# Reordering one DMA queue's window of loads in a two-batch Mamba block with adaptive layer norm

## The chip, the cores and the metric

The kernel runs on one core of one Trainium2 chip. The metric is the device time of one execution in microseconds (us). Five engines matter here: TensorE (PE in the profile; PEld is its weight load), VectorE (DVE), ScalarE (ACT), GpSimd (POOL) and SyncE (SP). SP computes nothing in this kernel. It is the queue on which nearly every DMA is issued, one after the other, each behind the semaphore waits written ahead of it.

## The reference

Input x is 2 batches of 2048 rows of 512. A small modulation vector gives shifts, scales and gates. Then two residual steps follow:

```
h = layernorm(x) * (1 + ca) + sa
x = x + ga * mamba(h)          # in_proj 512->2x1024, conv of 4 taps, silu, x_proj, dt_proj, softplus,
                               # scan s = s*exp(dt*A) + dt*h*B over time for 1024 channels x 16 states,
                               # y = sum_n s*C + h*D, y *= silu(gate), out_proj 1024->512
h = layernorm(x) * (1 + cb) + sb
x = x + gb * (sum_r h @ factors[r] / sqrt(8) + bias)
```

All data is float32.

## The kernel before, in words

The rows are cut into 16 chunks of 256 rows (`CHUNKS`), eight for each batch. Every engine's program is a loop over 16 rounds, one a chunk. In round c the four compute engines do the scan of chunk c, 64 units of two channel tiles by one state. They go through it in 32 steps (`s`) of two units. Woven into the same steps are the front part of chunk c+1 (input projection, convolution, silu, the dt, B and C projections) and the back part of chunk c-1 (gate, output projection, second norm and linear layer). What runs at which step is written out by hand for each engine.

The scan of a unit goes as follows. ACT makes the decay into one of three PSUM banks (L724). POOL makes dt*h*B for four units at a time (L570). DVE runs the scan (L1432). The product with C is made by DVE for some units (`sc_d`, a ring of three tiles, L1447) and by POOL for the others (`state_p`, L598). PE transposes and sums all products into `y_bank` (L1012).

PE's program at steps 1 to 7 of a round is what the change bears on. At s = 1, 2, 3, 4 and then 7, 8, 9, 10 it runs `project_h(c+1, q, j)` (L1087), which needs weight tile m = 2q + j of the input projection in `win_h`, a ring of three tiles. At s = 0, 1, 2 it ends the gate projection of chunk c-1 (`project_gate`, L1059, weight tiles in `win_z`, also a ring of three). At s = 4, 5, 6, 7 it runs `turn_sums(c-1, q)` (L1143). Behind each `turn_sums` DVE has a `gate_sums` (L1528): two at s = 6, one at s = 7, one at s = 8. At s = 6 PE runs the first convolution taps (L1070). ACT waits for them at s = 7 before its tanh.

The weight tiles do not stay in SBUF. For each chunk SP loads all eight `win_h` tiles (`load_h`, L359) and all eight `win_z` tiles (`load_z`, L371), 256 KB each. Because the rings hold three tiles, the load of tile m waits until the tile three before it has been used: `load_h(c+1, 3)` waits for `project_h` of tile 0 (s = 1), `load_z(c, 2)` waits for `project_gate` of the last tile of chunk c-1 (s = 2). SP further loads the B and C rows of a chunk, broadcast to all partitions (`load_b` L337, `load_c` L347, 1 MB a half), the input rows for the first norm (`load_xa`, L434, 512 KB) and for the residual (`load_xc`, L428, 512 KB), and stores the output (`store_out`, L501). SP's order is fixed by its `one_round` (L436 on); a wait there holds back everything written after it.

Of the kernel before, what the change touches and what calls it, by code (L numbers as in the profile page):

```python
# [34 lines left out]
KE = E // P  # L35
# [17 lines left out]
H_TILES, Z_TILES = 3, 3  # L53
# [65 lines left out]
def products_after(unit):  # L119
    return DVE_COUNT[unit]  # L120
# [41 lines left out]
def build(nc, x, win_m, xp_t, dt_t, wo_t, chan, cond_t, wmod, factors, bias, out):  # L162
# [11 lines left out]
    with ExitStack() as ctx:  # L174
# [144 lines left out]
        def _(sp):  # L319
# [5 lines left out]
            def store_bc(c, par):  # L325

                sp.wait_ge(a_free[1], A_FREES * c + 4)
                sp.dma_start(bc_dram[par].rearrange("i (n r) -> (i n) r", n=N), bc_s[:, :]).then_inc(bc_stored, 16)

            def load_b(c, par, h):  # L330

                if c:
                    sp.wait_ge(ub_made, QUADS * c - 2 * (1 - h) - 1)
                sp.wait_ge(bc_stored, 16 * c + 16)
                n0 = h * N // 2
                src = bc_dram[par, 0:1, n0 * ROWS:(n0 + N // 2) * ROWS].to_broadcast([P, N * ROWS // 2])
                sp.dma_start(b_all[:, n0:n0 + N // 2, :].rearrange("p n r -> p (n r)"), src).then_inc(b_loaded[h], 16)  # L337

            def load_c(c, par, h):

                if c:
                    sp.wait_ge(multiplied, products_after(UNITS * c - (1 if h else N // 2 + 1)))
                    sp.wait_ge(pooled, QUADS * c - 2 * (1 - h))
                sp.wait_ge(bc_stored, 16 * c + 16)
                n0 = h * N // 2
                src = bc_dram[par, 1:2, n0 * ROWS:(n0 + N // 2) * ROWS].to_broadcast([P, N * ROWS // 2])
                sp.dma_start(c_all[:, n0:n0 + N // 2, :].rearrange("p n r -> p (n r)"), src).then_inc(c_loaded[h], 16)  # L347

            def load_h(c, m):
                i = KE * c + m  # L350
                if c == CHUNKS:
                    return
                if i >= H_TILES:
                    (c0, m0) = divmod(i - H_TILES, KE)
                    if m0 % 2:
                        sp.wait_ge(a_full[m0 // 2 % 2], A_JOBS[m0 // 2 % 2] * c0 + 2 + m0 // 4)
                    else:
                        sp.wait_ge(h_used, PAIRS * c0 + m0 // 2 + 1)
                sp.dma_start(win_h[i % H_TILES][:, :, :], win_m[m]).then_inc(h_loaded[i % H_TILES], 16)  # L359

            def load_z(c, m):
                i = KE * c + m
                if i >= Z_TILES:
                    (c0, m0) = divmod(i - Z_TILES, KE)
                    if m0 % 2 and c0 == FINAL:
                        sp.wait_ge(a_full[m0 // 2 % 2], a_jobs + 1 + m0 // 4)
                    elif m0 % 2:
                        sp.wait_ge(c_full[m0 // 2 % 2], C_JOBS * c0 + 1 + m0 // 4)
                    else:
                        sp.wait_ge(z_used, PAIRS * c0 + m0 // 2 + 1)  # L370
                sp.dma_start(win_z[i % Z_TILES][:, :, :], win_m[KE + m]).then_inc(z_loaded[i % Z_TILES], 16)  # L371
# [41 lines left out]
            def store_wo(i):  # L413

                sp.wait_ge(wo_kept, i + 1)
                sp.dma_start(wo_dram[i], spare[2].rearrange("p t d -> p (t d)")).then_inc(wo_stored, 16)

            def store_ffn(i):

                sp.wait_ge(ffn_kept, i + 1)  # L420
                sp.dma_start(ffn_dram[i], spare[0].rearrange("p t d -> p (t d)")).then_inc(ffn_stored, 16)

            def load_xc(c):

                if c == 0:
                    sp.wait_ge(ffn_scaled, HALVES)
                wait(sp, out_stored, 16 * c)
                sp.dma_start(xc[:, :, :], rows_of(x_rows, c)).then_inc(xc_loaded, 16)  # L428

            def load_xa(c):  # L430

                for j in range(2):
                    sp.wait_ge(a_full[j], A_JOBS[j] * (c - 1) + 1)
                sp.dma_start(xa[:, :, :], rows_of(x_rows, c)).then_inc(xa_loaded, 16)  # L434

            def one_round(c, par, la, lc):  # L436
                if c >= 2:
                    store_out(c - 2)
                if c:
                    load_z(c - 1, 7)  # L440
                load_z(c, 0)
                if la is not None:
                    load_h(c + 1, 3)
                if c:
                    load_c(c, par, 1)
                load_z(c, 1)
                if la is not None:
                    load_h(c + 1, 4)
                load_z(c, 2)
                if la is not None:  # L450
                    load_h(c + 1, 5)
                    load_h(c + 1, 6)
                if c >= 2:
                    load_xc(c - 1)
                if c + 2 < CHUNKS:
                    load_xa(c + 2)
                if c == PER + 1:

                    sp.wait_ge(c_full[0], C_JOBS * PER)
                    sp.wait_ge(c_full[1], C_JOBS * PER)  # L460
                    sp.wait_ge(ffn_stored, 16 * HALVES)
                    sp.dma_start(ffn[:, :, :].rearrange("p (i k) d -> p i (k d)", i=HALVES),
                                 ffn_dram.rearrange("i p f -> p i f")).then_inc(ffn_loaded, 16)
                if la is not None:
                    load_h(c + 1, 7)
                    if c == 1:
                        store_ffn(0)
                    for m in range(H_TILES):
                        load_h(c + 2, m)
                    if c == 1:  # L470
                        store_ffn(1)
                        load_xc(0)
                    if c == 0:

                        sp.wait_ge(rows_made, 2 * BATCH)
                        for b in range(BATCH):
                            sp.dma_start(bias_gate[b:b + 1, :], gb[0:1, b, :]).then_inc(bias_gated, 16)
                        for i in range(PAIRS):
                            store_wo(i)
                    if c == PER:  # L480

                        sp.wait_ge(c_full[0], C_JOBS * (PER - 1) + 5)
                        sp.wait_ge(c_full[1], C_JOBS * (PER - 1) + 5)
                        sp.wait_ge(wo_stored, 16 * PAIRS)
                        sp.dma_start(wo[:, :, :].rearrange("p (i k) d -> p i (k d)", i=PAIRS),
                                     wo_dram.rearrange("i p f -> p i f")).then_inc(wo_loaded, 16)
                    store_bc(c + 1, 1 - par)
                    load_b(c + 1, 1 - par, 0)
                for m in (3, 4):
                    load_z(c, m)  # L490
                if la is not None:
                    load_b(c + 1, 1 - par, 1)
                    load_c(c + 1, 1 - par, 0)
                for m in (5, 6):
                    load_z(c, m)

            def store_out(c):

                for t in range(LB):
                    sp.wait_ge(c_free[t], C_JOBS * (c + 1))  # L500
                sp.dma_start(rows_of(out_rows, c), xc[:, :, :]).then_inc(out_stored, 16)  # L501

            rounds(one_round)
            load_z(FINAL, 7)
            store_out(FINAL - 1)
# [1230 lines left out]
```

## Time and profile before

| | us |
|---|---|
| median of 3 runs | 2046.96 |
| lowest, highest | 2046.85, 2053.15 |
| the profiled execution, its own time | 2046.96 |
| span of that execution in the trace | 2045.2 |
| busy in the span: DVE, POOL | 1865.8 (91%), 1834.8 (90%) |
| busy in the span: PE, ACT | 1775.0 (87%), 1514.3 (74%) |
| DMA queue of SP, share of 16 engines | 24.9% |

The time is the slowest (here the only) core's. The span runs from the first to the last instruction in the trace. The 1.8 us between the two lie outside it. A round lasts about 122 us. Engine busy shares are averages over the whole span, so they don't say what is waited for in a given step; the rows below do. Line numbers are those of the kernel before. Times in a row of the timeline are from the start of the span. A row may merge several like instructions (x4, x8), and square brackets hold the engine's idle time ahead of the row and what ended it. A row of windows gives the stretch, its length, then the busy time (and instructions) of PE, PEld, DVE, ACT and POOL in this order, then the granted clock of PE as a share of full speed, the busy share of the DMA engines and GB/s. A row of DMA issues ends with the KB of one and the us from issue to landing.

### The profile page before, as it was taken

Reading aid. Unit: us, or ns where it says so; the run is one execution under the profiler, and the core shown is the slowest. Engines: PE = TensorE matmul, PEld = TensorE weight load, DVE = VectorE, ACT = ScalarE, POOL = GpSimd, SP = SyncE. Lnnn points to the kernel's source line nnn. Section 1 sums busy time; section 2 is a strip of 40 time slices with the busy share of each in tenths; the row PEclk is TensorE's granted clock in tenths of the full one; section 3 lists DMA queues with packets and bytes.
Section 4 is the critical chain, followed back from the end, with each engine's and each line's share of the span. In section 5 each row is a group of like instructions: output and inputs, shape, how many; then the busy total and the mean of one; then the engine's idle time right before and its main releaser. Section 6 shows DMA issues by size and latency. Waiting matters only on the chain. (4 is left out here: it accounts for less than half of the span.)

```text
span 2045.2 us, 29343 instructions
## 1 busy us (share of the span) xinstructions
PE 1775.0 (87%) x9128; PEld 1317.7 (64%) x9128; DVE 1865.8 (91%) x2240; ACT 1514.3 (74%) x4646; POOL 1834.8 (90%) x925
## 2 busy tenths in 40 slices
PE   7976988989888888998989898898988889898698
PEld 5655757666575766757566675766657576675564
DVE  2899999999999999899999999999999999999995
ACT  3767778787877868678786877878687786877663
POOL 1789999998999999899999989999999999999992
PEclk9898999999999999999999999999999999999898
DMA  4656404032130402204032240403214040220300
GB/s 169 248 103 175 125 32 159 17 135 62 64 132 20 158 21 104 93 27 160 12 145 86 90 135 22 156 20 130 67 60 137 22 155 21 104 68 28 118 27 31
DMA packets 72001, 186.17 MB, mean 91 GB/s; under 512 B 6818, under 2 KB 8482, under 8 KB 63908
## 3 DMA queue, kind: packets, MB, share of 16 engines
q1 hardware_dynamic: 68148, 176.95, 24.9%
q0 software_dynamic: 3696, 7.34, 2.2%
q8 instruction: 73, 1.20, 0.2%
q14 instruction: 84, 0.69, 0.1%
HBM read 172.20 MB, written 12.06 MB: 90 GB/s over the span
## 5 line engine op out<-in xcount | busy, mean ns | idle before, releaser
L570 POOL TENSOR_TENSOR ub<-u,b_all 128x2048 f32<-128x2048 f32 x255 | 1160.3, 4550 | 46.7 <-DMA b_all<-bc_scratch 45.5
L724 ACT ACTIVATE decay<-dt,decay_rate 128x256 f32<-128x256 f32 (+1 forms) x2048 | 889.6, 466 | 32.9 <-DVE state_p L1432 30.5
L1432 DVE TENSOR_TENSOR_SCAN decay<-decay,carry,ub 128x512 f32<-128x512 f32 x610 | 761.9, 1276 | 27.2 <-ACT decay L724 26.1
L598 POOL TENSOR_TENSOR state_p<-state_p,c_all 128x1024 f32<-128x1024 f32 (+1 forms) x256 | 498.9, 1949 | 110.4 <-ACT carry L708 108.8
L1432 DVE TENSOR_TENSOR_SCAN state_p<-decay,carry,ub 128x512 f32<-128x512 f32 x414 | 527.5, 1274 | 20.3 <-ACT decay L724 18.6
L1012 PE MATMUL y_bank<-ident,sc_d 128*128 128x128 f32 x2440 | 367.3, 286 | 96.3 <-DVE sc_d L1447 96.0
L1012 PEld LDWEIGHTS y_bank<-ident,sc_d 128*128 128x128 f32 x2440 | 298.7, 148 | 175.9 <-DVE sc_d L1447 142.7
L1447 DVE TENSOR_TENSOR sc_d<-decay,c_all 128x512 f32<-128x512 f32 x610 | 407.0, 671 | 4.0 <-DMA c_all<-bc_scratch 3.9
L708 ACT ACTIVATE carry<-decay 128x2 f32<-128x2 f32 x610 | 100.6, 165 | 322.8 <-DVE sc_d L1447 322.8
L1012 PE MATMUL y_bank<-ident,state_p 128*128 128x128 f32 x1656 | 234.4, 281 | 52.4 <-POOL state_p L598 51.2
L1012 PEld LDWEIGHTS y_bank<-ident,state_p 128*128 128x128 f32 x1656 | 193.9, 144 | 123.6 <-POOL state_p L598 99.2
L1087 PE MATMUL bank_a<-hT,win_h 128*128 128x256 f32 x992 | 238.5, 384 | 24.4 <-DVE hc L1496 22.1
L1059 PE MATMUL bank_c<-hT,win_z 128*128 128x256 f32 x960 | 231.0, 387 | 0.0
L1159 PE MATMUL bank_c<-wo,yg 128*128 128x512 f32 x480 | 223.3, 593 | 0.0
L1087 PEld LDWEIGHTS bank_a<-hT,win_h 128*128 128x128 f32 x992 | 182.2, 192 | 48.7 <-DVE hc L1496 25.4
L1059 PEld LDWEIGHTS bank_c<-hT,win_z 128*128 128x128 f32 x960 | 182.3, 194 | 29.7 <-issue 6.7
L1159 PEld LDWEIGHTS bank_c<-wo,yg 128*128 128x128 f32 x480 | 85.2, 190 | 66.0 <-issue 64.6
L1189 PE MATMUL bank_c<-ffn,hT 128*128 128x512 f32 x240 | 125.8, 627 | 0.0
L1070 PE MATMUL bank_a<-pre_z,tap_diag 128*128 128x256 f32 x496 | 118.8, 382 | 1.9 <-DVE bank_a L1487 1.9
L1003 PE MATMUL y_bank<-ident,skipped 128*128 128x128 f32 x256 | 42.8, 293 | 80.9 <-ACT y_rows L813 80.9
L1070 PEld LDWEIGHTS bank_a<-pre_z,tap_diag 128*128 128x128 f32 x496 | 92.7, 192 | 26.1 <-issue 13.4
L720 ACT ACTIVATE decay<-ident 128x1 f32<-128x1 f32 x608 | 103.4, 170 | 0.1
(139 smaller groups left out, 1844.4 us busy)
## 6 DMA issues: line engine op xcount, KB each, us to landing
win_h<-win_m SPq DMA_DIRECT2D x128, 256.0 KB, 2.7
win_z<-win_m SPq DMA_DIRECT2D x128, 256.0 KB, 2.8
b_all<-bc_scratch SPq DMA_DIRECT2D x31, 1024.0 KB, 4.7
c_all<-bc_scratch SPq DMA_DIRECT2D x31, 1024.0 KB, 6.6
xa<-x SPq DMA_DIRECT2D x16, 512.0 KB, 5.1
xc<-x SPq DMA_DIRECT2D x16, 512.0 KB, 3.8
out<-xc SPq DMA_DIRECT2D x15, 512.0 KB, 3.8
ffn<-factors POOLq DMA_DIRECT2D x7, 1024.0 KB, 10.4
```

The lines of the kernel that those rows point to most:

```text
L570: pool.tensor_tensor(ub[:, slot, :, :, :], u[:, (PAIRS * c + q) % U_PAIRS, :, :].unsqueeze(1).to_broadcast([P, QUAD, 2, ROWS]), b_all[:, n ...
L598: pool.tensor_tensor(part, part, c_all[:, n + QUAD - k:n + QUAD, :].unsqueeze(2).to_broadcast([P, k, 2, ROWS]), ALU.mult).then_inc(pooled, 1)
L720: act.activation(bk[:, ROWS:ROWS + 1], ident[:, 0:1], ACT.Copy, scale=0.0)
L724: last = act.activation(bk[:, j * ROWS + j:(j + 1) * ROWS], dt[:, pair % DT_PAIRS, j, j:], ACT.Exp, scale=decay_rate[:, e, n:n + 1])
L1012: last = pe.matmul(y_bank[:, at:at + P], tile[:, j, t * P:(t + 1) * P], ident[:, :], start=False, stop=last_of_pair, is_transpose=True, sk ...
L1059: last = pe.matmul(dst[:, j * ROWS:(j + 1) * ROWS], tile[:, k, :], hTc[:, k, :], start=(k == 0), stop=(k == KD - 1))
L1070: last = pe.matmul(h_lane(c, q)[:, j * ROWS:(j + 1) * ROWS], tap_diag[:, i, 2 * q + j, :], pre[q % 2][:, j, k:k + ROWS], start=False, stop ...
L1087: last = pe.matmul(h_lane(c, q)[:, j * ROWS:(j + 1) * ROWS], win_h[i % H_TILES][:, k, :], hT[c % H_RING][:, k, :], start=(k == 0 and j == ...
L1159: last = pe.matmul(bank_c[t][:, :], yg[:, k, t * P:(t + 1) * P], wo[:, k, :], start=(k == 0), stop=(k == KE - 1))
L1189: last = pe.matmul(bank_c[t][:, :], hT[c % H_RING][:, k, t * P:(t + 1) * P], ffn[:, k, :], start=False, stop=(k == KD - 1))
L1432: dve.tensor_tensor_scan(dst, bk[:, :], ub[:, quad % UB_RING, i, :, :].rearrange("p j r -> p (j r)"), carried_in[:, n, 2 * q:2 * q + 1], A ...
L1447: dve.tensor_tensor(sc_d[:, i % D_RING, :, :], bk[:, :].rearrange("p (j r) -> p j r", j=2), c_all[:, n:n + 1, :].to_broadcast([P, 2, ROWS] ...
```

## The change

Only SP's `one_round` is altered. The loads and stores are the same ones, with the same waits, sizes and counts. Their order at the start of a round changes: the second half of C and the last gate tile come first, then the store of the finished chunk, then the gate tiles 0 to 2, then the rows for the residual and for the norm (and in one round the reload of `ffn`). Only then come the `win_h` tiles 3 to 7, which before were placed in between.

```
             def one_round(c, par, la, lc):
+                if c:
+                    load_z(c - 1, 7)
+                    load_c(c, par, 1)
                 if c >= 2:
                     store_out(c - 2)
-                if c:
-                    load_z(c - 1, 7)
-                load_z(c, 0)
-                if la is not None:
-                    load_h(c + 1, 3)
-                if c:
-                    load_c(c, par, 1)
-                load_z(c, 1)
-                if la is not None:
-                    load_h(c + 1, 4)
-                load_z(c, 2)
-                if la is not None:
-                    load_h(c + 1, 5)
-                    load_h(c + 1, 6)
+                for m in range(Z_TILES):
+                    load_z(c, m)
                 if c >= 2:
                     load_xc(c - 1)
                 if c + 2 < CHUNKS:
                     load_xa(c + 2)
...
                 if la is not None:
-                    load_h(c + 1, 7)
+                    for m in range(H_TILES, KE):
+                        load_h(c + 1, m)
                     if c == 1:
                         store_ffn(0)
                     for m in range(H_TILES):
```

SP's rows of one middle round before, from the gate tiles 5 and 6 that end a round (the first row holds these two) to the `win_h` tiles of the next; `out<-xc` is the store, `xc<-x` and `xa<-x` the two loads of rows:

```order
L371 DMA win_z<-win_m 128x512 x2
L501 DMA out<-xc 128x2x512
L371 DMA win_z<-win_m 128x512 x2
L359 DMA win_h<-win_m 128x512
L347 DMA c_all<-bc_scratch 128x2048
L371 DMA win_z<-win_m 128x512
L359 DMA win_h<-win_m 128x512
L371 DMA win_z<-win_m 128x512
L359 DMA win_h<-win_m 128x512 x2
L428 DMA xc<-x 128x2x512
L434 DMA xa<-x 128x2x512
L359 DMA win_h<-win_m 128x512 x4
```

The same stretch of SP's program after the change, whose first row is those two gate tiles and tile 7:

```order
L371 DMA win_z<-win_m 128x512 x3
L347 DMA c_all<-bc_scratch 128x2048
L493 DMA out<-xc 128x2x512
L371 DMA win_z<-win_m 128x512 x3
L428 DMA xc<-x 128x2x512
L434 DMA xa<-x 128x2x512
L359 DMA win_h<-win_m 128x512 x8
```

The first `win_h` load of the round, tile 3, stood ahead of `c_all` and of the gate tiles 1 and 2. It now stands behind all of them and behind both loads of rows. `c_all` and the gate tile 7 moved to the front, and the store behind them.

## Rows read from the trace of the kernel before

**Rows 1.** Busy by window in us: round 4, then round 1.
```profile
569.00:691.00 122.00, 107.16 (x566) 79.74 (x565) 114.42 (x138) 94.04 (x289) 114.07 (x59) 0.99 0.24 83
199.00:326.00 127.00, 108.59 (x563) 80.78 (x563) 116.49 (x142) 95.14 (x296) 122.95 (x66) 0.97 0.33 103
```

**Rows 2.** Waits of DVE, whole span: us in total, times, longest.
```profile
DVE sc_d L1447 <- DMA c_all<-bc_scratch: 3.9, 6, 1.4
```

**Rows 3.** SP's issues at the start of round 4: start, length, us.
```profile
570.12 2.06 SPq L371 DMA_DIRECT2D win_z<-win_m  x2
576.96 0.33 SPq L359 DMA_DIRECT2D win_h<-win_m  x1
577.39 0.37 SPq L347 DMA_DIRECT2D c_all<-bc_scratch  x1
578.68 0.33 SPq L371 DMA_DIRECT2D win_z<-win_m  x1
...
582.58 0.33 SPq L371 DMA_DIRECT2D win_z<-win_m  x1
...
585.61 2.49 SPq L359 DMA_DIRECT2D win_h<-win_m  x2
...
588.68 0.41 SPq L434 DMA_DIRECT2D xa<-x  x1
```

**Rows 4.** From issue to landing: those of 576.96, 578.68, 587.77 and 588.68.
```profile
win_h<-win_m SPq DMA_DIRECT2D x1, 256.0 KB, 3.3
...
win_z<-win_m SPq DMA_DIRECT2D x1, 256.0 KB, 5.1
...
win_h<-win_m SPq DMA_DIRECT2D x1, 256.0 KB, 2.5
...
xa<-x SPq DMA_DIRECT2D x1, 512.0 KB, 5.1
```

**Rows 5.** PE's timeline, round 4, steps 2 to 7.
```profile
580.65 1.89 PE L1059 MATMUL bank_c<-hT,win_z 128*128 128x256 f32 x8
...
585.86 1.89 PE L1087 MATMUL bank_a<-hT,win_h 128*128 128x256 f32 x8
...
589.33 0.60 PE L1143 MATMUL bank_c<-ident,y_rows 128*128 128x128 f32 x4
...
597.12 1.99 PE L1087 MATMUL bank_a<-hT,win_h 128*128 128x256 f32 x8 [1.71 <-DVE hc L1496]
```

**Rows 6.** DVE's timeline: twice round 4, then rounds 6 and 13.
```profile
583.25 0.69 DVE L1447 TENSOR_TENSOR sc_d<-decay,c_all 128x512 f32<-128x512 f32 x1 [0.90 <-DMA c_all<-bc_scratch]
...
591.65 1.28 DVE L1528 TENSOR_TENSOR yg<-bank_c,yg 128x512 f32<-128x512 f32 x2
...
834.82 1.28 DVE L1528 TENSOR_TENSOR yg<-bank_c,yg 128x512 f32<-128x512 f32 x2
...
1682.72 1.27 DVE L1528 TENSOR_TENSOR yg<-bank_c,yg 128x512 f32<-128x512 f32 x2
```

**Rows 7.** SP's issue of gate tile 2 in rounds 6 and 13.
```profile
825.26 0.33 SPq L371 DMA_DIRECT2D win_z<-win_m  x1
...
1674.66 0.33 SPq L371 DMA_DIRECT2D win_z<-win_m  x1
```

**Rows 8.** POOL's last product of round 3.
```profile
568.25 1.26 POOL L598 TENSOR_TENSOR state_p<-state_p,c_all 128x512 f32<-128x512 f32 x1
```

**Rows 9.** Gate tile 2 of round 1: issue to landing, us.
```profile
win_z<-win_m SPq DMA_DIRECT2D x1, 256.0 KB, 8.1
```

**Rows 10.** PE after two idle stretches.
```profile
562.69 0.66 PE L1012 MATMUL y_bank<-ident,sc_d 128*128 128x128 f32 x4 [2.60 <-DVE sc_d L1447]
...
665.53 0.63 PE L1003 MATMUL y_bank<-ident,skipped 128*128 128x128 f32 x4 [2.32 <-ACT y_rows L813]
```

**Rows 11.** Windows at 562.69 and after 665.53, with the granted clock.
```profile
558.00:569.00 11.00, 7.52 (x48) 6.39 (x47) 10.70 (x11) 10.13 (x34) 8.37 (x7) 1.00 0.79 305
...
666.60:670.00 3.40, 3.40 (x12) 2.25 (x11) 3.40 (x5) 2.17 (x8) 3.24 (x6) 0.50 0.00 0
```

## The prediction

> **What bounds the kernel now.** I read the busy time by window first, for a middle round. In 122 us DVE is busy 114.42 and POOL 114.07, against 107.16 for PE [rows 1]. So DVE has about 7.6 us of idle time in a round, and what holds DVE up in the middle of a round is passed on to the end almost whole. Then I read DVE's waits. The only DMA that DVE waits for in the steady rounds is the second half of C, 3.9 us in 6 waits [rows 2]. That is all this change could win from DVE directly. Then I followed SP's queue, PE and DVE through the first seven steps of round 4, because only there the order of the issues changes.
>
> Before, the weight tile 3 (call it h3) is issued at 576.96, right after `project_h` of tile 0, and lands 3.3 us later, at 580.3 [rows 3, 4]. PE uses it at 585.86 [rows 5]. It is 5.6 us early. In SP's queue the second half of C follows at 577.39 [rows 3] and lands when DVE's product at 583.25 is let go, after a wait of 0.90 us [rows 6].
>
> **The change, part by part.**
>
> *C earlier.* The load waits for the last products of the round before. POOL's ends at 569.5 [rows 8], and gate tile 7, which stays ahead of it, is issued at 570.12 [rows 3]. So C goes out at about 570.5, 6.9 us earlier, and DVE no longer waits for it. On its own this is worth at most the 3.9 us of [rows 2]. These waits lie ahead of the place where I find the loss, and that place is tied to PE and the DMA, not to DVE's earlier work. So I count the gain as nothing where the loss below occurs. Bounds: 0 to -3.9 us.
>
> *Store later, gate tiles together.* The store goes out at about 571, behind C. It has until about 583, when the load into its buffer is reached, so `out_stored` holds nobody back. Gate tiles 1 and 2 keep their own waits on PE and their times, 578.68 and 582.58 [rows 3]. Nobody needs tiles 0 to 2 before step 26. Price 0.
>
> *The `win_h` tiles later.* This is the term that counts. h3 now stands behind gate tile 2, and that waits for PE's last gate matmul. That one starts its run at 580.65 and is 1.89 us long [rows 5], so SP is free at 582.58. Behind it come the two loads of rows, 512 KB each, and only then h3. With the spacing of SP's issues (0.43 to 0.53 us) h3 goes out at about 584.0. But issue is not landing. The transfers of this queue land in order and share one path. The gate tile issued at 578.68 took 5.1 us and landed at 583.8, just 0.55 us behind C [rows 3, 4, 6]. So a queued 256 KB costs about 0.6 us. For the rows I take the same three transfers as they run before. The `win_h` load that ends the pair of 585.61 is issued at 587.77 and lands after 2.5 us at 590.3. The row load of 588.68 lands after 5.1 us at 593.8 [rows 3, 4]. From the first issue to the landing of the second row load that is 6.0 us, of which 3.5 are the two row loads. After the change gate tile 2 stands in that first place. I take 6.15, since landings are given to a tenth only and the first of the three may be slowed by what is ahead of it, and 0.65 for h3 behind: **h3 lands 6.8 us after the issue of gate tile 2**, here at 589.4, instead of 580.3. PE wants it at 585.86 and so stands still for 3.5 us.
>
> What is queued behind that wait on PE: the four matmul pairs of tile 3, `turn_sums` 0, the turns of step 5, `turn_sums` 1 (which starts 3.47 us after the tile-3 matmuls do and is 0.60 long, so it is done 4.07 us after h3 is in), then the taps [rows 5]. DVE waits for the two `turn_sums` with its two `gate_sums` of step 6. They start at 591.65, and the second at 592.25 (two in 1.28 us, [rows 6]). With h3 at 589.4 the second can start at 589.45 + 4.07 = 593.5, which is 1.3 us later. The first is let go at 591.8, no loss. The next things behind it have room: PE's tile 4 waits 1.71 us for DVE anyway [rows 5]. The taps (eight like matmuls, 1.89 us as the other rows of eight in [rows 5]) end at about 595.3, ACT's tanh and the copies behind them are some 3 us of work before the next decay that DVE needs two units later, so that they are in time by an estimated 1 us. So round 4 loses 1.3 us at full clock.
>
> The same sum for the twelve rounds 2 to 13: issue of gate tile 2 + 6.8 + 4.1 minus the start of the second `gate_sums`. The least is round 6, 825.26 + 10.9 against 835.4, 0.7 us [rows 6, 7]. The most is about that of round 13, 1674.66 + 10.9 against 1683.3, 2.25 us [rows 6, 7]. The twelve average 1.85. Together **22 us**.
>
> - Round 9 has the 1 MB reload of `ffn` ahead of h3 as well. By the 3.5 us of the two row loads this is another 3.5, less what rounding leaves: +3 us.
> - Round 14 has no load for the norm; 1.75 less, so about +0.5.
> - In round 1 gate tile 2 takes 8.1 us to land [rows 9], 5.3 more than the usual 2.8 of the page, so h3 is up to 4.9 us too late for DVE (1.3 + 5.3 - 1.75, no load for the residual yet). But there POOL is busy for 122.95 of 127 us [rows 1] and DVE has room against it. Bounds 0 and +4.9; I take +1.5.
> - Rounds 0 and 15: in round 0 h3 still waits for `project_h` of tile 0; in 15 there is none. 0.
>
> Sum at full clock 22 + 3 + 0.5 + 1.5 = 27 us.
>
> *The clock.* PE now stands still for about 3.5 us in each of these rounds. Rows show both answers: after 2.60 us idle PE went on at 1.00 (2.4 GHz), after 2.32 us its clock was 0.50 (1.2 GHz) for 3.4 us from 666.60 [rows 10, 11]. The new stand is longer than both. If PE resumes at half clock, the 4.07 us between h3 and `gate_sums` grow by up to 1.7 us (half of 3.4). Bounds 0 and 13 x 1.7 = 22 us. Since a drop may begin in the idle time and may stay out, I take 8.
>
> The Trainium skill ("TensorE: Matmul & The Clock Gate", section on HAM oscillation) says that a loop in which PE waits for a DMA between its bursts falls back to the half clock each time. By that rule the clock term would be at its upper end, 22 us. The trace agrees after the 2.32 us and not after the 2.60.
>
> **Sum:** the profiled execution took 2046.96 us, the median of the runs itself, with 1.8 us outside the span. 2047 + 27 + 8 = **2082 us**, 1.7% slower.
>
> **The rivals.**
>
> *A. Late, and as priced* (forecast): 2070 to 2092.
>
> *B. The burst lands early and only the gain is left.* This decides at one point: h3 must be there 4.07 us ahead of the second `gate_sums`, in round 4 at 588.2, which is 5.6 us after gate tile 2's issue instead of 6.8. If the loads of rows overlapped h3 so that it landed 2.7 us after its own issue, it would be in at 586.7 and nobody would be late. The waits for C go: 2047 - 3.9 = 2043. Against it: the landings in order, 0.55 us apart, in [rows 3, 4, 6]. The skill ("DMA: Bandwidth & Descriptors", Anatomy of one DMA) gives 2.0 us plus bytes over 436 GB/s. For the 1.5 MB from gate tile 2 to h3 this makes 5.6 us as an estimate, just at the point, and by it most rounds would lose well under 1 us; the rows here show 6.0 for 1.25 MB, slower than its 5.0, and I go by them.
>
> *C. Every resumption is at half clock:* 27 + 22 = 49, so 2096.
>
> *D. DVE makes good half of it.* DVE has 7.6 us of idle time in a round [rows 1], and if half the delay falls into waits that end on POOL or ACT work that was not delayed, 27 becomes 14: 2061. Against it: most of those waits end on ACT, which itself follows DVE.
>
> **How the numbers follow.** A 0.62, C 0.12, D 0.14, B 0.12. No change means within 0.3%, 6 us, about what a measurement of this kernel can tell. B is nearly all "same" (2043 is 0.2% less), with a little for faster. So faster 0.03, same 0.09, slower 0.88. The range leaves out B and the far end of C: 2058 to 2098.
>
> **What would show it.** In the profile after: h3's issue at about 14 us into a round's start instead of 7; a new wait of PE's L1087 for DMA `win_h`, 13 to 14 times, 3 to 4 us each, about 45 to 50 us in all, longest in round 9 or 1; a new wait of DVE's L1528 for PE L1143, some 22 us or more; DVE's wait for `c_all` gone; more stretches of PEclk 0.5. The prediction is wrong if L1087 waits for the DMA less than 2 us a time, or if DVE's L1528 does not wait although PE does.

## The result, and the profile after

The changed kernel takes 2102.22 us in the median of 4 runs (2098.09 to 2106.25), against 2046.9 before. The ratio is 1.0265, with a 95% interval of 1.0231 to 1.03: slower by 2.65%, where 1.7% was forecast, and 4 us beyond the upper end of the range. The direction and the mechanism were as forecast; the size was not.

The profiled execution took 2098.99 us, with a span of 2097.3 us, 52.1 more than before. The first lines of its page:

```profile
span 2097.3 us, 29343 instructions
...
PE 1794.1 (86%) x9128; PEld 1338.2 (64%) x9128; DVE 1866.6 (89%) x2240; ACT 1514.9 (72%) x4646; POOL 1833.7 (87%) x925
```

DVE, ACT and POOL do the same work in the same busy time. PE is busy for 19.1 us longer with the same 9128 matmul records: it ran a larger part of them at half clock (the mean granted clock of the span is 0.955, against 0.968 before). So the 52 us are idle time of DVE and POOL. The waits say which; first DVE's, then PE's for a DMA (us in total, times, longest):

```profile
DVE yg L1520 <- PE bank_c L1135: 62.1, 27, 6.0
...
DVE hc L1488 <- ACT tanh_s L781: 20.9, 16, 2.1
```

```profile
PE bank_a L1079 <- DMA win_h<-win_m: 53.4, 14, 6.6
```

(`gate_sums` is L1520 now, `turn_sums` L1135, `project_h` L1079, the gate projection L1051.) Neither the 62.1 nor the 53.4 us were in the trace before, and the wait of DVE for `c_all` [rows 2] is gone. The wait of `hc` was there, with 23.8 us. The 62.1 us are 10 more than the span grew; 3.9 of these are the waits for C. The other 6 are smaller waits of DVE that shrank, such as that of `hc`. So little of the delay was made good.

Round 4 again, SP's issues as in [rows 3]:

```profile
581.93 0.33 SPq L371 DMA_DIRECT2D win_z<-win_m  x1
582.37 0.37 SPq L347 DMA_DIRECT2D c_all<-bc_scratch  x1
582.84 0.39 SPq L493 DMA_DIRECT2D out<-xc  x1
583.66 10.48 SPq L371 DMA_DIRECT2D win_z<-win_m  x3
594.18 0.43 SPq L428 DMA_DIRECT2D xc<-x  x1
594.71 1.31 SPq L434 DMA_DIRECT2D xa<-x  x1
596.07 8.03 SPq L359 DMA_DIRECT2D win_h<-win_m  x4
```

The last row holds tile 3, issued at 596.07, with tiles 4 to 6. From issue to landing, the second load of rows and tile 3:

```profile
xa<-x SPq DMA_DIRECT2D x1, 512.0 KB, 5.8
...
win_h<-win_m SPq DMA_DIRECT2D x1, 256.0 KB, 5.1
```

So tile 3 is in at 601.2, 0.6 us behind the rows. PE and DVE in that stretch, as in [rows 5, 6]:

```profile
601.18 2.56 PE L1079 MATMUL bank_a<-hT,win_h 128*128 128x256 f32 x8 [3.93 <-DMA win_h<-win_m]
603.53 1.06 PE L1135 MATMUL bank_c<-ident,y_rows 128*128 128x128 f32 x4
604.38 1.78 PE L1004 MATMUL y_bank<-ident,state_p 128*128 128x128 f32 x8
606.00 0.60 PE L1004 MATMUL y_bank<-ident,sc_d 128*128 128x128 f32 x4
606.43 0.60 PE L1135 MATMUL bank_c<-ident,y_rows 128*128 128x128 f32 x4
...
611.96 0.48 PE L1079 MATMUL bank_a<-hT,win_h 128*128 128x256 f32 x1 [1.01 <-DVE hc L1488]
```

```profile
604.63 0.69 DVE L1520 TENSOR_TENSOR yg<-bank_c,yg 128x512 f32<-128x512 f32 x1 [2.68 <-PE bank_c L1135]
607.07 0.69 DVE L1520 TENSOR_TENSOR yg<-bank_c,yg 128x512 f32<-128x512 f32 x1 [1.75 <-PE bank_c L1135]
```

PE stands (sits idle, waiting) for 3.93 us, and then its eight records of tile 3, two for each of four matmuls, take 2.56 us instead of 1.89 and the transposes behind them 1.06 instead of 0.60. The windows from tile 3's first matmul to the second `gate_sums`, in rounds 4, 5 and 6, show the granted clock of each:

```profile
601.18:607.07 5.89, 5.89 (x29) 5.38 (x30) 1.46 (x3) 1.08 (x4) 5.81 (x6) 0.71 0.22 66
726.79:733.64 6.85, 6.85 (x29) 6.02 (x30) 1.46 (x3) 1.08 (x4) 6.77 (x6) 0.61 0.15 48
853.60:857.81 4.21, 4.21 (x29) 3.95 (x30) 1.75 (x3) 1.12 (x5) 4.13 (x5) 1.00 0.34 85
```

At clock 1.00 the same 29 matmul records take 4.21 us, which is the 4.07 of the forecast and the hand-over to DVE; at 0.71 they take 5.89 and at 0.61 they take 6.85. I read this stretch in all 14 rounds that wait: 4.2 us in rounds 6, 12 and 14, 5.9 in rounds 2, 4, 8 and 10, 6.3 in round 1, and 6.9 to 7.1 in the six odd rounds 3 to 13. Over 4.2 that is 25 us in all. The clock was low for 50.5 us of these stretches, and half of that is the same 25.

The stretch is 5.9 us or about 7 by how long the clock stays low. These are the low stretches of rounds 4 and 5:

```profile
602.48:605.89 3.41, 3.41 (x16) 3.04 (x15) 0.69 (x1) 0.58 (x2) 3.41 (x3) 0.50 0.28 76
725.36:732.18 6.82, 5.39 (x17) 4.56 (x18) 2.89 (x4) 2.27 (x8) 6.74 (x6) 0.50 0.31 109
```

In round 4 the clock fell 1.3 us after PE had gone on, and stayed low for 3.4 us. In round 5 it fell 1.4 us before PE went on, while PE stood, and stayed low for 6.8 us, 5.4 of them behind the wait.

### The profile page after: what moved, and what is told of

Read it like the earlier page. It is cut to its first block, busy times and chain, and to the rows that moved or that the text cites. A ratio compares the mean times of both kernels' runs of the same rounds, so it can differ in the third digit from the quotient of the medians.

```text
span 2097.3 us, 29343 instructions
## 1 busy us (share of the span) xinstructions
PE 1794.1 (86%) x9128; PEld 1338.2 (64%) x9128; DVE 1866.6 (89%) x2240; ACT 1514.9 (72%) x4646; POOL 1833.7 (87%) x925
## 4 chain that ended last, share of the span: by engine, by line
PE 16%; DVE 11%; ACT 9%; issue 7%; POOL 6%; DMA 2%; SPq 0%; DVEq 0%; ACTq 0%; POOLq 0%
DVE decay L1424 4%; PE bank_a L1079 4%; PE y_bank L1004 3%; ACT decay L716 3%; POOL ub L562 3%; DVE state_p L1424 3%; POOL state_p L590 3%; DVE sc_d L1439 2%; DMA win_h<-win_m 2%; PE bank_c L1051 2%; PE bank_c L1151 1%; PE bank_c L1181 1%; ACT dt L829 1%; ACT hT L731 1%; PE bank_a L1062 1%
## 5 line engine op out<-in xcount | busy, mean ns | idle before, releaser
L1079 PE MATMUL bank_a<-hT,win_h 128*128 128x256 f32 x992 | 254.0, 403 | 69.4 <-DMA win_h<-win_m 53.4
L1004 PE MATMUL y_bank<-ident,state_p 128*128 128x128 f32 x1656 | 240.1, 286 | 41.3 <-POOL state_p L590 40.2
L1004 PEld LDWEIGHTS y_bank<-ident,state_p 128*128 128x128 f32 x1656 | 202.0, 148 | 109.0 <-POOL state_p L590 82.0
L1079 PEld LDWEIGHTS bank_a<-hT,win_h 128*128 128x128 f32 x992 | 190.2, 201 | 99.9 <-DMA win_h<-win_m 56.7
L1051 PE MATMUL bank_c<-hT,win_z 128*128 128x256 f32 x960 | 232.5, 389 | 0.0
L1051 PEld LDWEIGHTS bank_c<-hT,win_z 128*128 128x128 f32 x960 | 183.1, 195 | 29.9 <-issue 6.7
L781 ACT ACTIVATE tanh_s<-bank_a 128x512 f32<-128x512 f32 x62 | 36.7, 592 | 123.3 <-PE bank_a L1062 122.8
```

The lines of the kernel that those rows point to most:

```text
L1004: last = pe.matmul(y_bank[:, at:at + P], tile[:, j, t * P:(t + 1) * P], ident[:, :], start=False, stop=last_of_pair, is_transpose=True, sk ...
L1051: last = pe.matmul(dst[:, j * ROWS:(j + 1) * ROWS], tile[:, k, :], hTc[:, k, :], start=(k == 0), stop=(k == KD - 1))
L1079: last = pe.matmul(h_lane(c, q)[:, j * ROWS:(j + 1) * ROWS], win_h[i % H_TILES][:, k, :], hT[c % H_RING][:, k, :], start=(k == 0 and j == ...
```

## The experiments

Each ratio is to runs of the kernel before taken beside the experiment. Their median was 2048 us for e1 to e4, 2049 us for e5 and e6 and 2051 us for e7 and e8.

**Only tile 3 moved back** (e1), from the changed kernel:

```
                 for m in range(Z_TILES):
                     load_z(c, m)
+                    if m == 0 and la is not None:
+                        load_h(c + 1, 3)
...
-                    for m in range(H_TILES, KE):
+                    for m in range(H_TILES + 1, KE):
```

> The changed kernel with one load moved back: weight tile 3 of the input projection stands behind gate tile 0 again, all else in the changed order. Theory (only tile 3 being late costs anything): PE waits for no win_h DMA in the rounds 2 to 14, DVE's wait of the gate_sums for PE falls from 62 us to under 2, and the time is that of the kernel before or up to 4 us less, 2043 to 2048. Rival (the store and the C load at the front, or tiles 4 to 7 behind the row loads, carry part of the loss): over 2060, with a new wait of PE for tiles 4 to 7.

2041.98 us, 1 us under the expected, ratio 0.997 (0.9957 to 0.9982). PE waits for no `win_h` load at all, and DVE for `turn_sums` once:

```profile
DVE yg L1522 <- PE bank_c L1137: 0.4, 1, 0.4
```

One load of 256 KB a round, at a wrong place, carries the whole loss. The store, C, the rows and the tiles 4 to 7 stayed where the change had put them.

**Only the tiles late** (e3), from the kernel before: `load_h(c+1, 3)` to `(c+1, 6)` taken out of their places and put, with tile 7, behind the loads of rows.

```
                     load_z(c - 1, 7)
                 load_z(c, 0)
-                if la is not None:
-                    load_h(c + 1, 3)
                 if c:
                     load_c(c, par, 1)
                 load_z(c, 1)
-                if la is not None:
-                    load_h(c + 1, 4)
                 load_z(c, 2)
-                if la is not None:
-                    load_h(c + 1, 5)
-                    load_h(c + 1, 6)
...
-                    load_h(c + 1, 7)
+                    for m in range(H_TILES, KE):
+                        load_h(c + 1, m)
```

> The kernel before with only tiles 3 to 6 moved behind the two loads of rows; the store and the C load keep their old places. Theory (the tiles carry all of it): about the changed kernel, 2095 to 2108, and DVE's waits for C, 3.9 us, stay or move. Rival (C and the store at the front carry a part of the 52 us): 2060 to 2085.

2107.39 us, ratio 1.0286 (1.026 to 1.0312), with the two waits of the changed kernel:

```profile
PE bank_a L1081 <- DMA win_h<-win_m: 57.1, 14, 6.3
```

```profile
DVE yg L1522 <- PE bank_c L1137: 61.9, 27, 6.3
```

With e1 this is both halves: the late tiles are enough for the loss, and tile 3 is needed for it. DVE's waits for C are gone here too, although C was not moved: DVE comes to them later.

**Tile 3 ahead of the rows** (e2), from the changed kernel: behind gate tile 2, but ahead of the two row loads.

```
                 for m in range(Z_TILES):
                     load_z(c, m)
+                if la is not None:
+                    load_h(c + 1, 3)
                 if c >= 2:
                     load_xc(c - 1)
...
-                    for m in range(H_TILES, KE):
+                    for m in range(H_TILES + 1, KE):
```

> The changed kernel with tile 3 directly behind gate tile 2 and ahead of the two loads of rows. Theory (the bytes in front of tile 3 are what makes it late, not the waits that its issue stands behind): tile 3 lands about 0.6 us behind gate tile 2, some 3.4 us after that one's issue, just when PE wants it; PE waits under 0.5 us a round, round 1 excepted; 2045 to 2052. Rival (standing behind the wait for the last gate matmul is the cost in itself): PE still stands 2 us or more a round, over 2070.

2044.54 us, ratio 0.9977 (0.9964 to 0.9991). The time is 0.5 us under the expected. PE's waits for the load are 7.0 us, most of it in round 1; the four others are of 0.2 to 0.9 us, where under 0.5 was expected:

```profile
PE bank_a L1081 <- DMA win_h<-win_m: 7.0, 5, 4.9
```

Tile 3 landed 3.2 to 4.3 us after the issue of gate tile 2 in rounds 2 to 14. So standing behind the wait for the last gate matmul costs nothing that the time shows; the 1 MB of rows in front does.

**One load of rows ahead** (e7): tile 3 between the two.

```
+                if la is not None:
+                    load_h(c + 1, 3)
                 if c + 2 < CHUNKS:
                     load_xa(c + 2)
...
-                    for m in range(H_TILES, KE):
+                    for m in range(H_TILES + 1, KE):
```

> The changed kernel with tile 3 between the two loads of rows: one load of 512 KB ahead of it instead of two. Theory (loss = lateness less DVE's room of about 1.7 us, plus half clock if PE stands long): tile 3 lands 5.0 to 5.4 us after gate tile 2 is issued, PE stands about 1.8 us in rounds 2 to 14, DVE waits 0 to 0.7 us a round there and up to 5 in round 1, the clock seldom drops behind so short a stand; DVE's wait for turn_sums is 6 to 14 us in all and the time 2046 to 2056. Rival (loss goes with the stand of PE, 1.8 of 3.6 us gives half of it): about 2072.

2059.15 us, ratio 1.0046 (1.0029 to 1.0063), about 9 us slower than before; the profiled one's span is 2059.0. The rival's 2072 is out, but my 2046 to 2056 was missed as well, and DVE's wait was 24.3 us instead of 6 to 14. The reason is mostly the clock: I had expected it to hold behind so short a stand. It was low for 21.1 us of the stretches up to the second `gate_sums`, in rounds 1, 3, 4, 11 and 12; less half of that, DVE's wait is 13.8 us, inside 6 to 14. Tile 3 also landed less evenly than expected, 4.7 to 6.7 us after gate tile 2 in rounds 2 to 14. Rounds 3 and 6, first PE, then the windows:

```profile
467.92 3.18 PE L1081 MATMUL bank_a<-hT,win_h 128*128 128x256 f32 x8 [1.88 <-DMA win_h<-win_m]
...
836.36 0.92 PE L1081 MATMUL bank_a<-hT,win_h 128*128 128x256 f32 x3 [1.80 <-DMA win_h<-win_m]
```

```profile
467.92:473.82 5.90, 5.90 (x29) 5.17 (x30) 3.51 (x5) 2.88 (x10) 5.82 (x5) 0.71 0.54 175
836.36:840.58 4.22, 4.22 (x29) 3.95 (x30) 3.50 (x5) 2.96 (x10) 4.14 (x4) 1.00 0.72 239
```

Two stands of like length, one followed by a drop and one not. In rounds where the clock held, DVE waited for 1.1 us less than PE had stood: 0.72 after 1.80, 0.38 after 1.46. That is DVE's room: so much later can PE's sums come without holding DVE up.

**PE late, but never idle** (e6), from the kernel before: 8 matmuls of zeros ahead of tile 3, whose loads keep their place. They add zero to a half bank that the next matmuls fill. The zero tile is written once, by GpSimd at the start.

```
+                if c >= 2 and 2 * q + j == 3:
+                    pe.wait_ge(zeroed, 1)
+                    for _ in range(8):
+                        pe.matmul(h_lane(c, q)[:, j * ROWS:(j + 1) * ROWS], zeros[:, :],
+                                  hT[c % H_RING][:, 0, :], start=False, stop=False, ...)
                 pe.wait_ge(h_loaded[i % H_TILES], 16 * (i // H_TILES + 1))
```

> The kernel before, its DMA order untouched, with 8 such matmuls of zeros ahead of tile 3: PE is late by 8 x 0.43 = 3.5 us at full clock, with no stand still and no DMA wait. Theory (lateness at full clock costs 3.5 us less the room that DVE has, about 1.7 us on the average, in 13 to 14 rounds): DVE waits 22 to 27 us more at the gate_sums and the time is 2068 to 2075. Rival (DVE makes good half of it later in the round): 2055 to 2062. Rival (lateness alone gives all the 52 us): 2090 or more.

2067.91 us, ratio 1.0099 (1.0072 to 1.0127), as the first theory had it, at the lower end of its 2068 to 2075. The zeros (two records for each matmul), tile 3 behind them, and the clock up to the second `gate_sums`:

```profile
590.17 3.62 PE L1091 MATMUL bank_a<-hT,zeros 128*128 128x256 f32 x16
593.63 1.89 PE L1095 MATMUL bank_a<-hT,win_h 128*128 128x256 f32 x8
```

```profile
593.60:597.70 4.10, 4.10 (x30) 3.82 (x30) 2.31 (x3) 1.69 (x6) 4.02 (x5) 1.00 0.19 59
```

```profile
DVE yg L1536 <- PE bank_c L1151: 26.0, 27, 1.5
```

Being 3.5 us late at full clock costs 20.6 us of span (2065.8 against 2045.2), not 52.

**The stand filled** (e5), from the changed kernel: the same edit with 7 matmuls of zeros, 3.0 us, ahead of the wait for the late tile 3.

> The changed kernel, with 7 matmuls of a zero weight tile (they add zero to the half bank that is filled next) on PE ahead of its wait for tile 3, in chunks 2 to 15. They take about 7 x 0.43 = 3.0 us, less than PE stood still there in nearly every round, so that PE is busy while it waits and tile 3 is used at the same time. Theory (about 26 of the 52 us are PE running at 1.2 GHz after the stand): the clock stays at 1.00 behind the wait, the stretch from the tile-3 matmuls to the second gate_sums is 4.2 us in all rounds instead of 4.2 to 7.1, DVE's wait for turn_sums falls from 62 us to about 36, and the time to 2070 to 2078. Rival (the drops would have come anyway, or matmuls of zeros do not hold the clock): 2095 or more, with the same drops.

2086.43 us, ratio 1.0191 (1.0166 to 1.0215) against 1.0265 for the changed kernel, whose intervals do not meet: more work for PE, and a faster kernel. Rounds 4 and 13, PE and then the windows:

```profile
598.75 1.99 PE L1087 MATMUL bank_a<-hT,win_h 128*128 128x256 f32 x8 [0.75 <-DMA win_h<-win_m]
...
1716.80 3.42 PE L1087 MATMUL bank_a<-hT,win_h 128*128 128x256 f32 x8 [1.92 <-DMA win_h<-win_m]
```

```profile
598.75:602.97 4.22, 4.22 (x29) 3.95 (x30) 1.62 (x4) 1.08 (x4) 4.14 (x5) 1.00 0.26 73
1716.80:1722.70 5.90, 5.90 (x29) 5.14 (x30) 0.69 (x1) 0.86 (x3) 5.90 (x3) 0.71 0.19 48
```

In 12 of the 14 rounds the stretch is 4.1 to 4.2 us at clock 1.00. Only in rounds 1 and 13, where PE still stood for 3.62 and 1.92 us, did it drop; in round 9 it held although PE stood for 2.69 us. But the time is above my 2070 to 2078, and DVE waits 47.1 us, not 36. Low clock in that stretch fell from 50.5 to 6.8 us, worth 22 us by half. Against this tile 3 landed 5 us later in the sum of the rounds (6.9 to 8.4 us after gate tile 2 in rounds 2 to 13, round 9 left out, against 6.4 to 7.3). The net 17 is near the 15 that DVE's wait fell by; of these the span shows 12 (2085.3 against 2097.3). Why the loads are slower in this kernel I did not find out.

**More filling** (e8): 9 matmuls, 3.9 us.

> The changed kernel with 9 matmuls of zeros ahead of the wait for tile 3 instead of 7: 9 x 0.43 = 3.9 us, so that PE hardly stands still at all and what is lost is lateness at full clock alone. Theory: no low clock between tile 3 and the second gate_sums except in round 1, DVE's wait for turn_sums 36 to 46 us, 2076 to 2086, not slower than with 7 although PE gets up to 0.9 us more work in front of tile 3 in some rounds. Rival (the filling itself delays tile 3 by as much as it saves): 2090 or more.

2085.64 us, ratio 1.0162 (1.0143 to 1.0181), DVE's wait 46.3 us. PE stands for 6.7 us in all, 2.33 of them in round 1 and 2.96 in round 9, where tile 3 landed 10.2 us after gate tile 2. In both rounds the clock fell; for round 9 I had not expected it. In the seven rounds in which the zeros cover the whole of the lateness DVE waits 2.44 us; that is 3.9 less a room of 1.45. From 7 to 9 matmuls nothing more is to be gained that this measurement tells apart.

**Only C first** (e4), from the kernel before:

```
             def one_round(c, par, la, lc):
+                if c:
+                    load_z(c - 1, 7)
+                    load_c(c, par, 1)
                 if c >= 2:
                     store_out(c - 2)
-                if c:
-                    load_z(c - 1, 7)
                 load_z(c, 0)
                 if la is not None:
                     load_h(c + 1, 3)
-                if c:
-                    load_c(c, par, 1)
                 load_z(c, 1)
```

> The kernel before with only the C load and gate tile 7 at the front of the round, the store behind them, the win_h tiles in their old places. Theory (the C waits of DVE are real but small): DVE's 3.9 us of waits for c_all go and the time is 2043 to 2047, 0 to 0.2% less than before. Rival (a later store or an earlier C collides with another transfer): 2050 or more, with a new DMA wait on some engine.

2041.67 us, 1.3 us under the expected, ratio 0.9974 (0.9961 to 0.9988). DVE waits for no `c_all` load any more, and the span is 2040.4 us, 4.8 less than before. So the first part of the change is good for 0.26% by itself. e4 and e1 are both faster than the kernel before, by a little that the intervals still show, and than the changed one; between the two nothing can be told.

## Why the prediction was right or wrong

- *What would break, and where.* Right. Tile 3 late behind the rows, PE standing at step 4, DVE at its two `gate_sums` of step 6. e1, e2 and e3 show that there is no second cause.
- *When tile 3 lands.* Forecast 6.8 us after gate tile 2 is issued, measured 6.4 to 7.3 in rounds 2 to 8 and 10 to 13, 9.2 in round 9, 4.8 in round 14, 10.0 in round 1. Right in the main, and it ruled out rival B. The estimate by the formula of the Trainium skill ("DMA: Bandwidth & Descriptors", Anatomy of one DMA), 5.6 us, was too low: the page gives it for one DMA issued by GpSimd, and here it was used for four in a row on SP's queue. e2 shows that an early landing would indeed have cost nothing.
- *Lateness at full clock.* Forecast 27 us after the 3.9 of C, so 31 of DVE's wait. Measured 62.1 less 25 of clock, 37. Short by 6. About 4 of these are round 1, taken at 1.5 with a bound of 4.9: PE stood there for 6.60 us and DVE for 7.4, 1.7 of it by the low clock, and the other 5.7 are outside the bound. About 2 are the landing, 7.0 us on the average of rounds 2 to 13 without round 9, not 6.8. The room of DVE came to about 1.7 us a round (3.5 less 1.85), read from the kernel before, where DVE had itself been held up on the way. In e1, without the waits for C, the second `gate_sums` starts 5.4 us after tile 3 does in rounds 2 to 14, which less 4.1 is a room of 1.3; e7 and e8 show 1.1 to 1.45. Over twelve rounds this comes to about 5 us, nearly all of it the 3.9 of C just counted.
- *The clock.* This is the step that failed. I took 8 us and bounded it at 22. It cost 25 us of DVE's wait. The bound came from one drop of 3.4 us per round. In the odd rounds 3 to 13 the low clock lasted for 6.8 us, long enough to cover nearly the whole stretch from tile 3 to the second `gate_sums`: 0.61 in the window of round 5, where a single such drop gives the 0.71 of round 4. The middle value rested on the hope that a drop would begin in the idle time and so cost less. In these six rounds it did begin there, 0.95 to 1.44 us before PE went on, and cost more: 2.6 to 2.9 us each, against 1.7 for the drops of rounds 2, 4, 8 and 10 that began behind it. e6 and e5 show that it is the stand that brings the drops, not the lateness: with PE late but busy there is none in 14 of 14 and 12 of 14 rounds.
- *Rival C*, every resumption at half clock, gave 2096 and named the right mechanism. It got 0.12 where it should have had most. The rule of the Trainium skill ("TensorE: Matmul & The Clock Gate", section on HAM oscillation) spoke for it: PE waits for a DMA in each round and falls back each time. The trace after agrees in 11 of 14 rounds; in 6, 12 and 14 the clock held.
- *Rival D*, DVE makes good half: wrong. Of 62.1 us of new waits 52.1 reached the span, and 3.9 of the rest are C.
- *The gain of C.* Right in size (3.9 forecast at most, 4.8 us of span in e4, and single runs of the kernel before differ by more than that) and right that the changed kernel would not see it: e3, without it, is at 1.0286 (1.026 to 1.0312) against 1.0265 (1.0231 to 1.03), which can't be told apart.

The sum as measured: 37 (late at full clock) + 25 (clock) - 3.9 (the waits for C, which have gone over into the 37) - 6 (other waits of DVE that shrank) = 52 us. Without the clock this is 27, the forecast to the microsecond, and that is partly luck: 6 too few for round 1 and the landing, 6 that other waits gave back. By this account the 17 us between 2082 and the 2099 of the profiled execution are the clock, 25 instead of 8; the median of the runs lies 3 us above that execution.

## What to carry to other kernels

In a queue whose loads land in order (in each of the ten traces here, all 409 DMAs of SP's queue landed in the order of their issue), count the bytes in front of each load up to the moment its data is wanted. Loads without a near deadline go behind those with one, and a load sorted by kind rather than by deadline cost this kernel 2.65%.

When PE will wait for a DMA, price the wait twice: once as lateness less the waiting engine's room, and once as half clock over the whole stretch behind it that others wait for, not over one drop of 3.4 us. If the DMA can't be made earlier, work that PE can do in the meantime can be worth it even when its result is thrown away (here 1.0191 against 1.0265), until the DMA is mended.

A reordering that mixes a good move with a bad one is best taken apart: C first alone gives 0.26%.

## What the runs showed of the hardware that was not expected

- The clock dropped behind stands of 1.88 us (e7) and 1.92 us (e5), and held behind 1.80 us and 2.07 us (e7), 2.69 us (e5), 3.63 us and 3.57 us (rounds 6 and 12 of the changed kernel). The length of the stand alone does not decide. What does was not settled. Counted over the 63 stands of PE for tile 3 of more than 0.3 us in the changed kernel, e2, e3, e5, e7 and e8, the clock was low in the stretch behind none of the 25 of up to 1.80 us, 6 of the 8 of 1.88 to 2.96 us, and 25 of the 30 of 3.04 us or more, with all 16 of 3.77 us or more among them.
- Matmuls with a zero weight tile held the clock at 1.00 as real ones do (e6: 14 of 14 rounds).
- Of the 31 drops behind these stands the 15 that began 0.85 us or more before PE went on lasted 6.8 us, and the 16 that began later, from 0.58 us before to 1.34 us after it, lasted 3.4 us.
- In the changed kernel the long drops came in round 1 and the odd rounds 3 to 13 and the short ones, or none, in the even ones. In e3, with tile 3 as late, they came in rounds 1, 7, 9, 11 and 12. So odd and even are no rule; why the drops began where they did is open.
